# Attention result projected in three products of high and low parts; stacked queries in a ring of five heads

## What is computed

```python
xn = layernorm(x)
q = xn @ w_q.T                       # 16 heads of 32
k, v = split(xn @ w_kv.T)            # one key and value head for all
q, k = rotate(q), rotate(k)
attn = softmax(where(causal, -max, q @ k.T))
out = (attn @ v).reshape(B, S, 512) @ w_proj.T + b_proj
x + out + shared_ffn(xn) + routed_experts(xn)
```

## Time and profile before

| | us |
|---|---|
| three timed runs | 1860.75, 1871.35, 1873.64; median 1871.35 |
| the profiled execution, whole | 1861.0 |
| its span | 1859.2 |
| attention stage, one batch without a pause | 121.6 |
| expert stage | 693 |

### The profile page before, as it was taken

How to read it: one execution, slowest core, us unless ns; L and a number is a source line. 1 busy time by engine, 2 the same in 40 slices (tenths; PEclk the granted TensorE clock), 3 DMA queues, 4 the chain that set the end, 5 groups by cost and what they waited for, 6 DMA issues and landing times.

```text
span 1859.2 us, 37173 instructions
## 1 busy us (share of the span) xinstructions
PE 1703.5 (92%) x10104; PEld 1370.8 (74%) x10104; DVE 1186.6 (64%) x3625; ACT 903.5 (49%) x2476; POOL 825.4 (44%) x670
## 2 busy tenths in 40 slices
PE   5833799999999999999999999999999999899999
PEld 5822676776767767777677676788888887788887
DVE  7778676767857766678587674455555554455557
ACT  2323574665747746657477475333333333233332
POOL 0042442433424423334244242577777766677760
PEclk9966899999999999999999999999999999999999
DMA  7984433433434334344343334688888888888794
GB/s 290 365 282 67 117 123 107 142 101 120 126 95 132 110 108 130 102 123 125 94 132 107 113 113 141 136 152 153 154 159 159 173 188 199 180 164 146 126 239 181
DMA packets 188936, 277.66 MB, mean 149 GB/s; under 512 B 34040, under 2 KB 130431, under 8 KB 186180
## 3 DMA queue, kind: packets, MB, share of 16 engines
q0 software_dynamic: 60352, 92.59, 24.6%
q1 hardware_dynamic: 73444, 117.19, 21.4%
q10 hardware_dynamic: 54944, 65.52, 11.6%
HBM read 123.93 MB, written 131.76 MB: 138 GB/s over the span
## 4 chain that ended last, share of the span: by engine, by line
PE 68%; DVE 12%; issue 6%; ACT 4%; DMA 3%; DVEq 1%; another core or an unknown queue 0%; POOL 0%; SPq 0%; ACTq 0%; POOLq 0%
PE e_psH L1518 12%; PE e_psY L1518 12%; PE m_psY L1217 6%; PE m_psT L1155 5%; PE m_psU L64 4%; PE m_psO L1173 4%; PE m_psU L66 4%; PE m_psU L65 4%; DVE m_sc L973 4%; PE e_psT L1532 3%; PE m_psS L1138 3%; PE e_psX L1507 3%; ACT m_sc L838 2%; DMA sums<-e_y,e_where 2%; DVE m_sc L983 2%
## 5 line engine op out<-in xcount | busy, mean ns | idle before, releaser
L1487 POOL DMA_INDIRECT sums<-e_y,e_where x287 | 445.4, 1552 | 220.4 <-DVE e_y L1446 71.1
L764 POOL DMA_INDIRECT slot_rows<-m_row,slots x256 | 269.3, 1052 | 593.8 <-ACT m_sc L838 541.2
L838 ACT ACTIVATE m_sc<-m_sc,m_low 128x512 f32<-128x512 f32 (+3 forms) x512 | 283.8, 556 | 179.9 <-DVE m_low L973 159.5
L973 DVE CUSTOM_DVE_ANT_0 m_sc<-m_psS,cst 128x512 f32<-128x512 f32 (+3 forms) x512 | 230.1, 485 | 133.5 <-PE m_psS L1138 128.1
L1518 PE MATMUL e_psH<-e_w,e_xt 128*128 x1148 | 296.4, 381 | 1.6 <-ACT e_xt L1389 1.6
L1518 PE MATMUL e_psY<-e_w,e_ht 128*128 x1148 | 296.6, 381 | 0.0
L1389 ACT ACTIVATE e_xt<-e_psX 128x256 f32<-128x256 f32 x287 | 110.2, 384 | 215.3 <-PE e_psX L1507 146.0
L1394 ACT ACTIVATE e_ht<-e_psT 128x256 f32<-128x256 f32 x287 | 110.3, 384 | 212.5 <-PE e_psT L1532 185.2
L1155 PE MATMUL m_psT<-cst,m_sc 128*128 128x128 f32 x1280 | 200.1, 278 | 13.8 <-ACT m_pt L849 13.3
L1518 PEld LDWEIGHTS e_psH<-e_w,e_xt 128*128 128x128 f32 x1148 | 196.3, 191 | 16.8 <-issue 1.8
L1518 PEld LDWEIGHTS e_psY<-e_w,e_ht 128*128 128x128 f32 x1148 | 196.6, 191 | 15.2 <-issue 0.3
(11 more groups left out here) (192 smaller groups left out, 3150.9 us busy)
## 6 DMA issues: line engine op xcount, KB each, us to landing
e_row<-slot_rows ACTq DMA_DIRECT2D x287, 144.5 KB
m_qs<-m_qhi SPq DMA_DIRECT2D x256, 64.0 KB, 2.0
e_w<-in_w SPq DMA_DIRECT2D x64, 256.0 KB
f_xt<-in_x SPq DMA_DIRECT2D x8, 1024.0 KB, 9.8
xnt_hi<-f_hi SPq DMA_DIRECT2D x8, 1024.0 KB, 4.4
xnt_lo<-f_lo SPq DMA_DIRECT2D x8, 1024.0 KB, 8.4
m_qs<-m_qlo SPq DMA_DIRECT2D x128, 64.0 KB, 2.0
sums<-empty POOLq DMA_DIRECT2D x32, 256.0 KB
```

The source lines that it names most:

```text
L764: pool.indirect_dma_start(out=xs, out_offset=bass.IndirectOffsetOnAxis(ap=slots_sb[:, g, k:k + 1], axis=0), in_=row[g % 2][:, :], in_offse ...
L838: nc.scalar.activation(cols, cols, ACT.Exp, bias=low[:, h % 2, i:i + 1], scale=-1.0, accum_out=total[:, h % 2, i:i + 1]).then_inc(exp_done, 1)
L973: nc.vector.tensor_tensor_reduce(out=sc[:, h % 2, SPC[i]:SPC[i] + n], in0=psS[k % 2][:, 0:n], in1=mask[:, S - n:S], scale=1.0, scalar=3.0e ...
L1487: pool.indirect_dma_start(out=both_sums, out_offset=bass.IndirectOffsetOnAxis(ap=where[u % NY][:, 0:1], axis=0), in_=y[u % NY][:, :], in_o ...
```

## The change

- The attention's result is projected by `three`. After the last values of a batch ScalarE makes `oh`, the rounding to float32r of all four feature chunks: three from `ot` and the last from the bank psO. VectorE makes `ol`, what is left, in four subtractions ahead of rotating q0. TensorE waits for `ol` before tile 0, and before it overwrites psO for the next batch's first four heads.
- The projection's weight is split once in batch 0: ScalarE makes `proj_hi` in slots 10 to 13, VectorE `proj_lo` one slot behind.
- `qs` is a ring of five heads (QR = 5) in place of two sets of four. Each head's moves wait for all scores of the head five before. `m_qlo` has the bytes of `m_q`: the low part is made in place, so ScalarE's copy into m_q waits until the moves of the set before have landed.
- `oh` and `ol` lie in the bytes of `m_pt` behind head 0's first two parts, and the front's tile xn in bytes that later tiles use.
- SP's batches are written out.

```diff
+QR = HC + 1
...
+PROJ_AT = 10
...
+        with ExitStack() as over:
+            q = over.enter_context(nc.sbuf_tensor("m_q", [P, S], F32))
...
-        qs = sb("m_qs", [96, 2, HC, S], F32R)
+        qs = sb("m_qs", [96, QR, S], F32R)
...
-        pt = sb("m_pt", [P, HC, NSP])
...
+            pt = over.enter_context(nc.sbuf_tensor("m_pt", [P, HC, NSP], F32))
+        sb("m_first", [P, HC * NSP - 2 * KC * S])
+        oh, ol = (sb(f"m_o{n}", [P, KC, S], F32R) for n in ("h", "l"))
...
+        def queries_before(b, name):
+
+            c = int(name[1:])
+            return before(b if c else b + 1, c)
...
-                sp.wait_ge(s_done, at(b, NH * TB, HC * TB * (c - 1)))
 
                 def move(j, k, src):
-                    sp.dma_start(qs[k * HD:(k + 1) * HD, c % 2, j, :].bitcast(F32),
+                    sp.dma_start(qs[k * HD:(k + 1) * HD, (b * NH + c * HC + j) % QR, :].bitcast(F32),
                                  src[j * HD:(j + 1) * HD, :].bitcast(F32)).then_inc(qs_in[c % 2][j], 16)
 
                 for j in range(HC):
+                    if b * NH + c * HC + j >= QR:
+                        sp.wait_ge(s_done, at(b, NH * TB, TB * (c * HC + j + 1 - QR)))
                     move(j, 0, qhi)
                     move(j, 1, qhi)
...
-            with sp.Fori(0, B - 1) as b:
-                turn(b, False)
-            turn(B - 1, True)
+            for b in range(B):
+                turn(b, b == B - 1)
...
+                    bb, cc = queries_before(b, name)
+                    for j in range(HC):
+                        act.wait_ge(qs_in[cc % 2][j], stacked(bb, cc))
...
+                    if c == KC - 1:
+                        for k in range(c):
+                            nc.scalar.activation(oh[:, k, :], ot[:, k, :], ACT.Copy).then_inc(oh_made, 1)
+                        act.sem_inc(o_out, 1)
+                        nc.scalar.activation(oh[:, c, :], psO[:, :], ACT.Copy).then_inc(oh_made, 1)
+                        return
...
+                    if first and PROJ_AT <= s < PROJ_AT + KC:
+                        act.wait_ge(proj_in, 16)
+                        c = s - PROJ_AT
+                        nc.scalar.activation(proj_hi[:, c, :], proj_raw[:, c, :], ACT.Copy).then_inc(proj_hi_made, 1)
...
+                    if first and PROJ_AT < s <= PROJ_AT + KC:
+                        c = s - PROJ_AT - 1
+                        dve.wait_ge(proj_hi_made, c + 1)
+                        nc.vector.tensor_tensor(proj_lo[:, c, :], proj_raw[:, c, :], proj_hi[:, c, :].bitcast(F32),
+                                                ALU.subtract).then_inc(proj_lo_made, 1)
...
+                for c in range(KC):
+                    dve.wait_ge(oh_made, b * KC + c + 1)
+                    nc.vector.tensor_tensor(ol[:, c, :], psO[:, :] if c == KC - 1 else ot[:, c, :], oh[:, c, :].bitcast(F32),
+                                            ALU.subtract).then_inc(ol_made, 1)
...
-                    pe.matmul(psS[k % 2][:, 0:n], qs[:, c % 2, h % HC, i * P:(i + 1) * P], ks[:, 0:n],
+                    pe.matmul(psS[k % 2][:, 0:n], qs[:, (b * NH + h) % QR, i * P:(i + 1) * P], ks[:, 0:n],
...
+                                if b > 0:
+                                    pe.wait_ge(ol_made, b * KC)
...
-                pe.wait_ge(o_out, at(b, KC, KC))
+                pe.wait_ge(ol_made, (b + 1) * KC)
                 if first:
-                    pe.wait_ge(proj_in, 16)
+                    pe.wait_ge(proj_lo_made, KC)
...
-                    mm = pe.matmul(psY[n % 2][:, :], ot[:, c, tok], wproj[:, c, :], start=(c == 0), stop=(c == KC - 1))
+                    mm = three(pe, psY[n % 2][:, :], (oh[:, c, tok], ol[:, c, tok]), (proj_hi[:, c, :], proj_lo[:, c, :]), c == 0, c == KC - 1)
```

More of the change, by code:

```diff
@@ L91, in pipeline, with front @@
                 step(turns, s - lag)
-def front(nc, x, consts, fc1g, xnt_hi, xnt_lo, rows, cst, logits, spare):
+def front(nc, x, consts, fc1g, xnt_hi, xnt_lo, rows, cst, logits, spare, xn):
     with ExitStack() as ctx:
@@ L109, in front @@
         xt = [sb(f"f_xt{u}", [P, TB, D]) for u in range(R)]
-        xn = sb("f_xn", [P, TB, D])
         hi = [sb(f"f_hi{u}", [P, KC, S], F32R) for u in range(R)]
@@ L626, in middle @@
             for pair, c in ((wq, KC), (wkv, KC), (wup, KC), (wdown, SC))]
+        proj_raw, proj_hi, proj_lo = wproj
         kv = sb("m_kv", [P, S])
-        q = sb("m_q", [P, S])
+        with ExitStack() as over:
+            q = over.enter_context(nc.sbuf_tensor("m_q", [P, S], F32))
+        qlo = sb("m_qlo", [P, S], F32R)
         rot = sb("m_rot", [P, S])
         qhi = sb("m_qhi", [P, S], F32R)
-        qlo = sb("m_qlo", [P, S], F32R)
-        qs = sb("m_qs", [96, 2, HC, S], F32R)
+        qs = sb("m_qs", [96, QR, S], F32R)
         ks = sb("m_ks", [96, S], F32R)
@@ L673, in middle @@
         pads_sent = sem("m_pads_sent")
-        proj_in = sem("m_proj_in")
+        proj_in, proj_hi_made, proj_lo_made = sem("m_proj_in"), sem("m_proj_hi_made"), sem("m_proj_lo_made")
+        oh_made, ol_made = sem("m_oh_made"), sem("m_ol_made")
         routing = Routing(nc, sb, sem, weights, bias, logits, rows, slots_sb, pads_sb, empty, xs, experts_dram, shifts_dram, cst,
@@ L721, in sp_program @@
             stack(0, 0, -1)
-            sp.dma_start(wproj[:, :, :].rearrange("p c n -> p (c n)"), wproj_dram).then_inc(proj_in, 16)
+            sp.dma_start(proj_raw[:, :, :].rearrange("p c n -> p (c n)"), wproj_dram).then_inc(proj_in, 16)
             sp.dma_start(bp[:, :], bproj.partition_broadcast(P)).then_inc(bp_in, 16)
@@ L1621, in build @@
         sems = ctx.enter_context(ExitStack())
+        with ExitStack() as over:
+            front_rows = over.enter_context(nc.sbuf_tensor("front_rows", [P, TB, D], F32))
         with ExitStack() as inner:
@@ L1631, in build @@
             empty = sb("empty", [P, ROW])
-            proj = sb("proj", [P, KC, D])
+            with ExitStack() as over:
+                front_spare, proj_raw = (over.enter_context(nc.sbuf_tensor(n, [P, KC, D], F32)) for n in ("front_spare", "proj_raw"))
+            proj_hi, proj_lo = (sb(n, [P, KC, D], F32R) for n in ("proj_hi", "proj_lo"))
             xh, xlo = (sb(n, [P, KC, S], F32R) for n in ("xh", "xlo"))
@@ L1636, in build @@
             front(nc, x, consts, w_fc1_gate, xnt_hi, xnt_lo, rows, cst, logits,
-                  proj[:, :, :].rearrange("p c n -> p (c n)"))
-            attention = middle(nc, sems, x, bproj, xnt_hi, xnt_lo, xh, xlo, rows, halves["wq"], halves["wkv"], proj, halves["wup"], halves["wdown"],
+                  front_spare[:, :, :].rearrange("p c n -> p (c n)"), front_rows)
+            attention = middle(nc, sems, x, bproj, xnt_hi, xnt_lo, xh, xlo, rows, halves["wq"], halves["wkv"], (proj_raw, proj_hi, proj_lo), halves["wup"], halves["wdown"],
                    cst, slots_sb, pads_sb, empty, slot_rows, sums, partial, logits, ot, gate_bias, experts_dram, shifts_dram, wproj,
```

## The result

| | before | after |
|---|---|---|
| median of 16 runs each | 1863.74 us | 1855.16 us |
| profiled execution, whole (span) | 1861.0 (1859.2) | 1852.67 (1850.9) |

The ratio of the times, after to before, is 0.9942 with a 95% interval of 0.9925 to 0.9960: some 11 us less of 1864 by the ratio, 8.6 by the medians, 8.3 in the profiled executions. The interval leaves out 1, so there is a gain, and a small one: it lies inside the 1% band. One of the sixteen runs of the changed kernel took 4334.74 us; no trace shows why, and the ratio leaves it out.

What follows compares the result with a forecast made beforehand. TensorE's queue was taken as the bound, except where VectorE's chain is as long. Terms -12.6 + 2.5 + 0.5 = -9.6 us, off a four-execution mean of 1866.7, gave 1857 us; range 1836 to 1877.

Steps and rivals of the forecast that it cites:

- The products: Result projection on TensorE: a tile takes 2.79 us instead of 3.43, 0.64 us shorter; 32 tiles free 20.5 us.
- The boundary: At each of seven batch boundaries 1.8 us of the freed TensorE time arrives, 12.6 us in all.
- The first rival: At the batch boundaries all that TensorE frees arrives, 18 us, end and weights for nothing: 1849 us; chance 0.15.
- The halves of the result: At batch boundaries, making oh and ol on ScalarE and VectorE costs nothing, with 0.5 us of cover.
- The second rival: At batch boundaries, subtractions over 0.5 us later than expected delay the scores; cover wholly gone, 2.5 us each: 1874 us; chance 0.17.
- The queries in place: ScalarE's query copy has 4.3 us in hand after the low part's moves land; ring waits cost nothing.
- The slower rival: Query copies of slots 4 and 8 wait for late transfers, costing 32 us: 1889 us; chance 0.06.
- The weight's halves: Batch 0, slots 10 to 14: four copies and four subtractions cost between 0 and 5.2 us, taken as 2.5.
- The end of the last batch: Behind the last batch nothing covers the halves: from -0.5 to +1.5 us, taken as +0.5.
- The sum of -9.6: Whole kernel: -12.6 us at boundaries, +2.5 for the weight's halves, +0.5 at the last batch's end.
- The chance of 0.17 for over 1% faster: Whole kernel 19 us faster or more: 0.07 from all freed time arriving, 0.10 from the forecast with few pauses.

Runs made afterwards that it cites:

- the quiet pair: Traces without "remote" pauses: the kernel before with only the query part of the change, 1822.39 us, and the whole changed kernel traced again, 1815.95 us.

## Why the prediction was right, and where it was off

Forecast was 1857 us, 0.5% under the mean of the four executions known then. Measured: 1855.16 us and 0.6% under before.

1. *The products*: 2.81 us a tile against 2.79. Right, and the full float32 tiles put the batch back at 120.0 us. The Trainium skill, "TensorE: Matmul & The Clock Gate", section "Back-to-back issue gap", gives 215.8 ns for 512 columns as the gap of an isolated matmul, and about 131 ns in a stream of pairs of weight load and matmul. Twelve products in 2.81 us are 234 ns each, so this trace agrees with neither, and the measured pitch had to be used. The prediction read the 215.8 ns as the price when nothing waits for the weights, and laid the other 17 ns to the weight loads; no run shows what they are.
2. *The boundary*: 1.8 us predicted, 1.81 measured, and piece by piece. Against the key's copy the first scores came 1.01 us earlier (0.95 predicted), the first mask 0.37 (0.3), tile 2 0.82 (0.83), the mask behind it 1.35 (1.47), that of slot 2 1.80. Four shorter tiles give 2.5 us; 0.7 stays with VectorE's chain, as worked out. The first rival, that all arrives, is out.
3. *The halves of the result*: predicted at nothing with 0.5 us of cover; 0.08 us and 0.56. The second rival had the right mechanism and asked for over 0.5 us more; the doubled subtractions bring it about, at 1.5 us a boundary in the six where the clock stayed up, less than the 2.5 that I had named for a cover gone wholly (the 0.56 us of cover and a part of the rest are taken up).
4. *The queries in place*: nothing, and alone nothing. In after the last move of the low part is issued at 599.16 and the query's copy follows at 605.86, released by TensorE:

```profile
599.16 0.59 SPq L719 DMA_DIRECT2D m_qs<-m_qlo  x1
...
605.86 0.60 ACT L824 ACTIVATE m_q<-m_psU 128x512 f32<-128x512 f32 x1 [0.93 <-PE m_psU L66]
```

   605.86 - 599.16 - 0.59 - 2.0 = 4.1 us in hand, against 4.3 predicted. The slower rival had no ground.
5. *The weight's halves*: 2.5 predicted, 2.7 at the masks. I had charged ScalarE's copies and VectorE's subtractions alike and halved the sum of 5.2, because half of the slots have a pause; which of the eight operations are covered I hadn't worked out, so the near hit owes something to luck. In fact one copy and three subtractions cost, 0.45, 0.60, 0.60 and 0.69 us: the copy because the query's rounding, on which VectorE waits, stands behind it, the subtractions because a mask was due at once. One subtraction stood in a pause and cost nothing, the other three copies show no loss of their own, and 0.35 us follow from the delay.
6. *The end of the last batch*: +0.5 within -0.5 to +1.5; measured +0.1 or +1.3, and 1.5 to 1.6 in two kernels with the weight's halves moved, by whether the clock falls behind the pause.

The sum of -9.6 stands against -12.6 + 2.7 + 0.1 = -9.8 from the traces at the full clock, or -8.6 at the low one. The spans of the quiet pair, where the clock fell in the changed kernel, differ by only -5.7, since the tail of batch 0 (+0.4), the late transfer (+1.2), the start (-1.0 up to slot 10) and the experts (+2.3) vary from trace to trace: the stretch of the experts, the same code in all, took 688 to 698 us in thirteen traces. The level was off by 3 us: the mean of four executions was 1866.7, the median of sixteen 1863.74, so a forecast right to 2 us owes part of that to luck. The batch of 121.6 us, taken for one without a pause, is 1.6 us longer than the 120.0 of the quiet traces; the gain in it was forecast right (119.8 against 121.6, measured 118.2 against 120.0). The chance of 0.17 for over 1% faster rested on executions with few pauses; but both kernels have them, and the ratio is 0.9942 where they are and 0.9959 in the set without them, within each other's intervals. So they belong in the range of the time, not in that of the ratio.

## What to carry to other kernels

An instruction added to an engine costs what the wait behind it was worth: four subtractions cost 0.08 us where the engine had stood 4.8 us, nothing was lost by one in a pause of 2 us, and 0.6 us by each where a mask was due at once; a copy on ScalarE cost 0.45 us because VectorE's next input came behind it. So cost an addition by its place, and where an addition can't be covered, as behind the last batch, let the consumer wait for each part and not for all. When two traces scatter by more than the effect, line them up on an event in each round of the loop: the 1.8 us were plain at every boundary although the batches differed by 4.

## What was not expected of the hardware

- The same pause of 3.28 us on TensorE was followed by the full clock in three traces and by a stretch at 1.2 GHz in three others, with the same kernel on both sides. Behind the shorter pauses there, 0.72 us in four traces and 1.57 us in two, the clock stayed at 1.00 in all. With the halves at the end of other slots the clock fell too, 1.5 us after the products had begun:

```profile
1107.60:1109.10 1.50, 1.45 (x6) 1.24 (x7) 0.00 (x0) 0.00 (x0) 0.00 (x0) 1.00 0.87 240
1109.10:1111.90 2.80, 2.80 (x8) 2.17 (x7) 0.00 (x0) 0.00 (x0) 0.00 (x0) 0.51 0.35 119
```

- The sets differ by 39 us, 2%, for the same kernel: 1823 against 1863 us. Some 12 us of it lie in batch 0 (155.6 and 156.3 us before, 143.8 with the queries alone), and 1 to 8 us in each later batch, partly at rows with "remote" of 0.15 to 6.5 us on ScalarE and VectorE, which the 1823 sets lack altogether. What those pauses are no row says. Each of the three sets ran on another chip, so whether the chip or something else sets the level isn't shown. Each ratio here is taken within one set.
